# One transformer layer on one core: the opening rewritten in one interleaved order

## What is computed

```python
x = L0_attn_h
xn = _layernorm(x, axis=-1)
x = x + _L0_attn_ref(xn, ...) + _L0_ffn_ref(xn, ...)

# _L0_attn_ref(h, ...)
mu = jnp.mean(h, axis=-1, keepdims=True)
var = jnp.mean(jnp.square(h - mu), axis=-1, keepdims=True)
x = (h - mu) * jax.lax.rsqrt(var + EPS) * ln_g + ln_b
q, k, v = x @ wq.T + bq, x @ wk.T + bk, x @ wv.T + bv   # then rope(q), rope(k)
attn = softmax(causal(q k^T * scale)); o = attn v
return o @ wo.T + bo + residual                         # residual = h

# _L0_ffn_ref(hidden_states, ...)
topk_idx, topk_w = _gate(x, gate_w, gate_bias)          # logits = x @ gate_w.T
out = _moe(x, topk_idx, topk_w, w1, w2, w3)
shared = jax.nn.silu(x @ shared_gate) * (x @ shared_up) @ shared_down
return (out + shared).reshape(b, s, h)
```

## Time and profile before

| | us |
|---|---|
| median of 3 runs | 1180.03 |
| lowest, highest | 1176.62, 1180.87 |
| the profiled execution | 1178.42 |
| its span in the trace | 1176.6 |

### The profile page before, as it was taken

How to read it: one execution, slowest core, us unless ns; L and a number is a source line. 1 busy time by engine, 2 the same in 40 slices (tenths; PEclk the granted TensorE clock), 3 DMA queues, 4 the chain that set the end, 5 groups by cost and what they waited for, 6 DMA issues and landing times.

```text
span 1176.6 us, 18983 instructions
## 1 busy us (share of the span) xinstructions
PE 1076.8 (92%) x6706; PEld 942.2 (80%) x6706; DVE 862.3 (73%) x1691; ACT 665.6 (57%) x1453; POOL 621.7 (53%) x480
## 2 busy tenths in 40 slices
PE   4735789998989999999999999999999999999996
PEld 3635678887778888888888888889888888888885
DVE  6457458898888998887766767676766666676785
ACT  3423456554656655565556656666656566666652
POOL 1045055544555555456475667566665657566541
PEclk9757799998989999999999999999999999999998
DMA  5041021111112211213233323332323223231122
GB/s 178 1 130 59 23 45 37 38 36 46 32 41 45 55 41 42 45 29 77 56 77 77 91 59 78 80 91 65 79 55 85 75 67 77 73 75 33 39 73 90
DMA packets 49613, 73.33 MB, mean 62 GB/s; under 512 B 12272, under 2 KB 26992, under 8 KB 49392
## 3 DMA queue, kind: packets, MB, share of 16 engines
q1 hardware_dynamic: 46192, 67.66, 22.0%
q0 software_dynamic: 3328, 4.46, 2.5%
HBM read 29.74 MB, written 8.80 MB: 33 GB/s over the span
## 4 chain that ended last, share of the span: by engine, by line
PE 79%; DVE 14%; ACT 2%; DMA 2%; issue 1%; POOL 1%; SPq 0%; DVEq 0%; ACTq 0%; POOLq 0%
PE ps L278 22%; PE ps L280 21%; PE ps L279 20%; PE ps L400 10%; PE ps L461 2%; DVE nmax L1246 2%; PE ps L390 1%; PE ps L473 1%; DVE acc L1279 1%; DVE k_l L980 1%; DVE q_l L980 1%; PE ps L319 1%; DMA fin_y<-token_sum 1%; DVE xn L1033 1%; DVE st L1019 1%
## 5 line engine op out<-in xcount | busy, mean ns | idle before, releaser
L1386 POOL TENSOR_TENSOR qb<-qb,k_sb 128x512 f32<-128x512 f32 x128 | 172.5, 1348 | 436.3 <-DMA qs<-qb 436.0
L865 ACT ACTIVATE prob<-ps,nmax 128x128 f32<-128x128 f32 (+7 forms) x256 | 190.5, 744 | 89.4 <-DVE nmax L1246 88.0
L1246 DVE TENSOR_REDUCE nmax<-ps 128x1 f32<-128x128 f32 (+7 forms) x256 | 190.7, 750 | 41.7 <-PE ps L390 40.6
L876 ACT ACTIVATE ptd_h<-ps 128x128 fp32r<-128x128 f32 (+3 forms) x256 | 108.7, 437 | 192.1 <-PE ps L400 191.9
L1390 POOL TENSOR_TENSOR qb<-qb,qs 128x512 f32<-128x512 f32 x128 | 184.7, 1443 | 18.6 <-POOL qs L1387 0.4
L400 PE MATMUL ps<-k_sb,prob 128*128 128x128 f32 x1152 | 178.9, 279 | 11.6 <-DVE ptr_l L1255 6.9
L1255 DVE TENSOR_TENSOR ptd_l<-ps,ptd_h 128x128 fp32r<-128x128 f32 (+3 forms) x256 | 123.8, 484 | 67.3 <-ACT ptd_h L876 65.9
L1387 POOL TENSOR_TENSOR qs<-qs,k_sb 128x512 f32<-128x512 f32 x128 | 172.4, 1347 | 0.0
L400 PEld LDWEIGHTS ps<-k_sb,prob 128*128 128x128 f32 x1152 | 136.4, 144 | 26.5 <-issue 13.3
L278 PE MATMUL ps<-k_h,q_h 128*128 128x512 f32 (+3 forms) x384 | 141.5, 369 | 13.1 <-DVE q_l L980 11.3
L280 PE MATMUL ps<-k_h,q_l 128*128 128x512 f32 (+3 forms) x384 | 133.2, 347 | 0.0
(11 more groups left out here) (163 smaller groups left out, 2735.7 us busy)
## 6 DMA issues: line engine op xcount, KB each, us to landing
qs<-qb SPq DMA_DIRECT2D x256, 128.0 KB, 2.3
ew<-epack SPq DMA_DIRECT2D x16, 768.0 KB
rqk<-wqk SPq DMA_DIRECT2D x16, 256.0 KB, 3.0
xt<-x SPq DMA_DIRECT2D x4, 512.0 KB, 4.9
rv<-wvp SPq DMA_DIRECT2D x8, 256.0 KB, 4.0
ro<-wop SPq DMA_DIRECT2D x16, 128.0 KB, 2.3
token_table<-xn SPq DMA_DIRECT2D x4, 512.0 KB, 4.1
token_sum<-xt SPq DMA_DIRECT2D x4, 512.0 KB, 3.1
```

The source lines that it names most:

```text
L865: act.activation(prob[:, t % 2, 0:w], score[t % 2][:, 0:w], ACT.Exp, bias=nmax[:, t:t + 1], accum_out=rsum[:, t:t + 1]).then_inc(exp_done, 1)
L876: act.activation(turned(0, t, j0, w), src, ACT.Copy).then_inc(pth_done, 1)
L1246: dve.tensor_reduce(nmax[:, t:t + 1], score[t % 2][:, 0:(t + 1) * P], AX.X, ALU.max, negate=True).then_inc(max_done, 1)
L1386: pool.tensor_tensor(qb[:, i, :], qb[:, i, :], cos_sb[:, c], ALU.mult).then_inc(rope_a, 1)
```

## The change

It rewrites the opening. Its parts:

1. *Order.* The stages are cut into pieces (`turn_x`, `turn_z`, `gate`, `shared`, `down` on TensorE; `x_hi`, `again`, `affine`, `z_hi`, `logits`, `shared_tanh`, `shared_hi`, `shared_out` on ScalarE; `stats`, `norm`, `x_lo`, `z_lo`, `shared_g`, `shared_u`, `shared_lo` on VectorE) and written in one interleaved order on all engines, with `pro_uses` to match. The projection of unit 1's first piece moves into it. The closing barrier goes; the scores of unit 0 wait for single banks.
2. *Norm.* The root is made on GpSimd: variance plus eps, power -0.5, a Newton step. `zz` is made on ScalarE as `rstd * xn - mean * rstd`.
3. *No base sum.* GpSimd's `rest` and the stores of the sum go. In unit 1 SP copies the rows of `token_table` to `token_sum` (2048 rows), and ahead of unit 4's rope GpSimd issues an accumulating DMA of x onto them; the first scatter waits for it. `bo` is put in row 0 of `cacc`, which is summed over partitions at the end anyway.
4. *Buffers.* `zz`, `xnh`, `xnl` and `sth` get two places, `sh` and `xnt` go, and statistics have a place for each norm. One of the two buffers of q and k moves in SBUF.
5. *Router product.* It is made of three products on split values (`gwh`, `gwl`), with `xnl` subtracted straight from PSUM.
6. *Loads.* The weights of the shared expert are loaded ahead of the small tables; x's chunks 2 and 3 wait for `xn_ready` alone, and stand ahead of the stores.

```diff
-        pro_uses = stage_a(0) + stage_a(1) + stage_b(0) + stage_a(2) + stage_b(1) + stage_a(3) + stage_b(2) + stage_b(3)
+        pro_uses = [
+            ("xt", 0, 0), ("xt", 0, 1), ("zt", 0, 0), ("zt", 0, 1), ("xt", 1, 0), ("g", 0, 0), ("xt", 1, 1), ("u", 0, 0),
...
+            ("zt", 3, 1), ("gate", 3), ("d", 3, 0), ("d", 3, 1)]
...
                 bank = popen("gate", q)
                 for i in range(GT):
                     for k in range(KC):
-                        ins = pe.matmul(bank[:, i * EXPERTS:(i + 1) * EXPERTS], xnt[:, k, i * P:(i + 1) * P],
-                                        gw[:, k, :], start=(k == 0), stop=(k == KC - 1))
+                        ins = three(pe, bank[:, i * EXPERTS:(i + 1) * EXPERTS],
+                                    (xnh[q % 2][:, k, i * P:(i + 1) * P], xnl[q % 2][:, k, i * P:(i + 1) * P]),
+                                    (gwh[:, k, :], gwl[:, k, :]), k == 0, k == KC - 1)
...
-                if n == 0 and t == 0:
-                    for i in range(4):
-                        pe.wait_ge(pro_free[i], len([u for u in range(len(pro_uses)) if u % 4 == i]))
+                if n == 0 and t in (0, 1, 4, 5):
+                    i = 2 * (t % 2) + t // 4
+                    pe.wait_ge(pro_free[i], len([u for u in range(len(pro_uses)) if u % 4 == i]))
...
             def more_x(q):
-                sp.wait_ge(base_out[q % 2], 16)
+                sp.wait_ge(xn_ready, q - 1)
                 sp.dma_start(xt[:, q % 2, :, :], x_t[q]).then_inc(x_in[q % 2], 16)
 
+            more_x(2)
             rows(0)
             load_rqk(sp, 1)
-            load_ro(sp, 1)
-            more_x(2)
+            more_x(3)
+            rows(1)
             swap(sp, 0, 0)
...
+                if n == 1:
+                    for p in range(2):
+                        sp.wait_ge(rows_out[p], 32)
+                    sp.dma_start(y[0:TOK, :], table[0:TOK, 0:DM]).then_inc(y_rows, 16)
...
+            def again(q):
+                act.wait_ge(root2_ready, q + 1)
+                if q >= 2:
+                    act.wait_ge(pro_done, pcount("zt", q - 2, 1))
+                for i in range(GT):
+                    ins = act.activation(zz[:, q % 2, i, :], xn[:, q % 2, i, :], ACT.Identity, bias=shift[:, q, i:i + 1],
+                                         scale=rstd[:, 2 * q + 1, i:i + 1])
+                ins.then_inc(z_ready, 1)
...
+            def root_of(q, s, nth):
+
+                j = 2 * q + s
+                pool.wait_ge(mv_ready, nth)
+                stepped(pool.tensor_scalar(var[:, j, :], mv[:, j, :, 1], EPS, None, ALU.add))
+                stepped(pool.tensor_tensor(root[:, j, :], var[:, j, :], power[:, :], ALU.pow))
+                stepped(pool.tensor_tensor(newton[:, j, :], root[:, j, :], root[:, j, :], ALU.mult))
+                stepped(pool.tensor_tensor(newton[:, j, :], newton[:, j, :], var[:, j, :], ALU.mult))
+                stepped(pool.tensor_scalar(newton[:, j, :], newton[:, j, :], -0.5, 1.5, ALU.mult, ALU.add))
+                if s == 0:
+                    pool.tensor_tensor(rstd[:, j, :], newton[:, j, :], root[:, j, :], ALU.mult).then_inc(root1_ready, 1)
+                    return
+                stepped(pool.tensor_tensor(rstd[:, j, :], newton[:, j, :], root[:, j, :], ALU.mult))
+                stepped(pool.tensor_tensor(shift[:, q, :], mv[:, j, :, 0], rstd[:, j, :], ALU.mult))
+                pool.tensor_scalar(shift[:, q, :], shift[:, q, :], -1.0, None, ALU.mult).then_inc(root2_ready, 1)
...
+            root_of(0, 0, 1)
+            root_of(1, 0, 2)
+            root_of(0, 1, 3)
+            root_of(1, 1, 4)
+            root_of(2, 0, 5)
+            pool.wait_ge(consts_in, 16)
             rope(pool, 0, 0)
             rope(pool, 0, 1)
-            rest(1)
+            root_of(3, 0, 6)
             rope(pool, 0, 2)
             rope(pool, 0, 3)
-            rest(2)
-            rest(3)
+            root_of(2, 1, 7)
+            root_of(3, 1, 8)
+
+            def base(m):
+                if m != 4:
+                    return
+                pool.wait_ge(y_rows, 16)
+                pool.dma_start(y[0:TOK, :], x, max_dma_last_dim=4 * DM, accum_op=ALU.add).then_inc(y_base, 16)
```

More of the change, by code:

```diff
@@ new lines, in shared @@
+            def shared(q, f, s):
+                for k in range(KC):
+                    pe.wait_ge(*freed("xt", q, k))
+                pe.wait_ge(swl_ready, s + 1)
+                bank = popen("gu"[s], q, f)
+                for k in range(KC):
+                    w = slice(k * FS + f * P, k * FS + (f + 1) * P)
+                    ins = three(pe, bank, (swh[:, s, w], swl[:, s, w]), (xnh[q % 2][:, k, :], xnl[q % 2][:, k, :]),
+                                k == 0, k == KC - 1)
+                ins.then_inc(pro_done, 1)
@@ new lines, in down @@
+            def down(q, i2):
+                pe.wait_ge(shl_ready, 2 * (q + 1))
+                pe.wait_ge(swl_ready, 3)
+                bank = popen("d", q, i2)
+                for i in range(2):
+                    t = slice((2 * i2 + i) * P, (2 * i2 + i + 1) * P)
+                    for f in range(2):
+                        w = slice(f * DM, (f + 1) * DM)
+                        ins = three(pe, bank[:, i * DM:(i + 1) * DM], (shh[:, f, t], shl[:, f, t]),
+                                    (swh[:, 2, w], swl[:, 2, w]), f == 0, f == 1)
+                ins.then_inc(pro_done, 1)
@@ L494, in _ @@
             pe.wait_ge(id_in, 16)
-            pro_a(0)
+            turn_x(0, 0)
+            turn_x(0, 1)
+            turn_z(0, 0)
+            turn_z(0, 1)
+            turn_x(1, 0)
+            shared(0, 0, 0)
+            turn_x(1, 1)
+            shared(0, 0, 1)
+            shared(0, 1, 0)
             project(0, 0)
             project(0, 1)
-            pro_a(1)
-            pro_b(0)
+            gate(0)
+            turn_z(1, 0)
+            turn_z(1, 1)
+            shared(0, 1, 1)
+            turn_x(2, 0)
+            gate(1)
+            turn_x(2, 1)
             project(0, 2)
             project(0, 3)
-            pro_a(2)
-            pro_b(1)
-            for f in range(4):
-                values(0, f)
-            pro_a(3)
-            pro_b(2)
-            pro_b(3)
+            shared(1, 0, 1)
+            shared(1, 0, 0)
+            values(0, 0)
+            shared(1, 1, 0)
+            down(0, 0)
+            down(0, 1)
+            shared(1, 1, 1)
+            values(0, 1)
+            gate(2)
+            shared(2, 0, 0)
+            values(0, 2)
+            project(1, 0)
+            turn_z(2, 0)
+            turn_x(3, 0)
+            shared(2, 1, 0)
+            turn_x(3, 1)
+            shared(2, 0, 1)
+            turn_z(2, 1)
+            shared(2, 1, 1)
+            down(1, 0)
+            down(1, 1)
+            shared(3, 0, 0)
+            shared(3, 1, 0)
+            down(2, 0)
+            down(2, 1)
+            shared(3, 0, 1)
+            shared(3, 1, 1)
+            turn_z(3, 0)
+            turn_z(3, 1)
+            gate(3)
+            values(0, 3)
+            down(3, 0)
+            down(3, 1)
             pe.wait_ge(maskb_ready, 1)
-            pe.wait_ge(pro_act, 1)
-            pe.wait_ge(pro_vec, 1)
-            project(1, 0)
             for n in range(UNITS):
@@ L811, in pro_d, with shared_tanh @@
[L811 to L820 removed]
+            def shared_tanh(q, f):
+                bank = drop("g", q, f)
+                if q:
+                    act.wait_ge(shl_ready, 2 * (q - 1) + f + 1)
+                act.activation(sth[:, f, :], bank, ACT.Tanh, scale=0.5).then_inc(tanh_ready, 1)
@@ L858, in _ @@
-            act.wait_ge(pro_vec, 1)
+            shared_out(3, 0)
+            shared_out(3, 1)
             def exps(n, t):
```

520 lines of the change are left out of this document (274 added, 246 removed), and 4 rows, old and new, of the table pro_uses.

## The result

| | median us | lowest, highest (runs) |
|---|---|---|
| before, measured beside it | 1178.32 | 1175.93, 1180.87 (4) |
| changed | 1116.42 | 1112.83, 1118.84 (4) |

The ratio is 0.9478, 95% interval [0.946, 0.9496]. The forecast was 1118 us, 1.6 above the median; the range held. The profiled execution took 1118.84 us, its span is 1117.0 us.

A forecast was written before the change was run, and what follows sets the result against it. It took the opening to be bound by waits between engines, the rest by TensorE's work. Lead-in 19.9, work 62.2, clock 3 and stalls 6 make 91.1 against 153.5 us, 62.4 less: 1118 us, range 1106 to 1142.

The forecast's parts named there:

- Lead-in: Start of the opening: statistics, two roots and norms until the first eight zz transposes end, at 19.9 us.
- TensorE's work, clock and stalls: Opening behind the lead-in: 62.2 us of work, 3 lost to clock at the stream's start, 6 of stalls (0 to 20).
- What leaves nothing: Removing the opening's base sum gains nothing by itself, its cost being off the new bound; likewise table reloads, barrier, doubled buffers.
- The root is paid once: GpSimd's slower root costs some 4 us at the very start only; later roots lie beside matmuls.
- VectorE 60, ScalarE 54, TensorE 62: Opening's summed work per engine in us; VectorE and ScalarE stay below TensorE's work plus lead-in.
- What comes back later: Units 1 to 4: the 2 MB copy and the 2 MB accumulating DMA, both costed at nothing.
- rival E: Around unit 4's ropes: GpSimd stands inside the accumulating DMA's issue, 88 us more, 1206 us, slower than before; chance 0.03.
- the prediction's own sign of being wrong: Wrong if the first score comes after 115 us, or units 1 to 5 grow by more than 5 us together.
- The rule of the page: Exclusive VectorE-GpSimd port lock: the opening's four ropes could raise VectorE's 60 us to 75, still under 91.
- B: Root chain in the opening is slow, each GpSimd step 1.26 us; 21 us more, 1139 us; chance 0.14.
- C: Opening's pieces do not interlock, 25 us of TensorE idle remain instead of 6; 1137 us; chance 0.13.
- D: Unit 1's copy holds up swaps, all 16 us reaching TensorE through a rope; 1134 us; chance 0.04.

The follow-up runs named there:

- base_behind: Changed kernel with the accumulating DMA of x issued behind unit 4's first rope piece instead of ahead of it; 1111.40 us, ratio 0.9438.
- sum_back: Changed kernel with the base sum and its stores put back into the opening, without the later copy and accumulating DMA; 1129.50 us, ratio 0.9587.
- no_newton: Changed kernel with accumulating DMA moved to unit 12 and copy to unit 9, and the root's Newton step left out; 1111.33 us, ratio 0.9434.
- gate_fp32: Changed kernel with the router's product as eight fp32 matmuls a chunk on xn's high part, instead of 24 on split values; 1110.99 us, ratio 0.9424.
- both_late: Changed kernel with the accumulating DMA moved from unit 4's rope to unit 12's and the token_table copy from unit 1 to 9; 1112.55 us, repeated 1112.27.
- stage_order: Changed kernel with all its parts, but every engine's queue written in the stage order of the kernel before; 1180.31 us, ratio 1.0025.

## Why the forecast was right, and where it was not

*Lead-in.* Forecast 19.9 us to the end of the first zz transposes, measured 21.2. The first root took 2.5 us for the forecast 2.6, but by two errors that cancel: simple steps at 0.28 and the power at 1.13, for 0.44 each. The second took 4.4 instead of 3.5, with wide VectorE operations beside it (0.57 for 0.24, 1.44 for 1.05, 0.63 for 0.24), and the four ScalarE operations behind it 2.07 for 1.6. No extra time for a first call showed: GpSimd starts on mv at 7.12, 0.2 us after it was done.

*TensorE's work, clock and stalls.* Forecast 62.2 + 3 + 6 = 71.2, measured 87.7 - 21.2 = 66.5 without a gap. The router's step was 0.11 as priced. The clock of 0.95 over these 66.5 us is 3.3 us lost, all of it from 30 to 45 us and not at the start of the stream, where the forecast put its 3. At the start the windows give a clock of 1.00, but the matmuls of 512 columns step 0.42 and 0.43 us from 22.46 to 23.31, as at half the clock, for 0.23 later; that is 1.1 us more. With 4.4 lost to the clock for the 3 taken, some 62 are left for the work, as forecast, and no stall at all: the term of stalls was 6 too large. 6 less of stalls against 1.3 more of lead-in and 1.4 more of clock make the 3.3 between 65.7 and 62.4. Stalls and clock were not independent here: in `base_behind`, whose opening is the same program, TensorE stands 1.2 us between 20 and 90 us at a clock of 0.98, and unit 0 starts at 88.13, where the changed kernel has 88.02.

*What leaves nothing.* This step failed, though the sum did not notice it. The prediction put the cost of the base sum on GpSimd and in VectorE's norm, "both off the new bound"; inside the new order, at the places it was given there, the sum costs 16 us at the first score (`sum_back`). It was right only that its removal had already been counted, since I followed the order through without it.

*The root is paid once.* This held for the kernel as it is: TensorE waits for no root behind the lead-in, and shorter chains (`no_newton`) give little more than their two of the lead-in, 2.3 to 3.6 us. It holds without a margin: six more steps a chain cost 11.3 us at the first score, not 4. TensorE is full from 20 to 90 us, but with 1.7 us more a chain chunk 2's norm already comes 2.9 us late. "VectorE 60, ScalarE 54, TensorE 62" compared sums, and a sum does not say that a round of one chunk fits between two places in the order. `gate_fp32` shows the same from the other side.

*What comes back later.* The accumulating DMA was priced at nothing, because GpSimd stands 343 us for swaps over the loop; rival E looked at GpSimd standing inside the issue. The issue took 2.17 us and the transfer 15.1, so rival E is out. What was missed is the third engine: an issue ahead of a rope changes when GpSimd's products run, and VectorE, whose q_l TensorE waits for in unit 2, stands beside them. In the profiled execution that is what the trace shows. That it is the cause of the two groups of times is not shown: the long execution of `base_behind` has no such operation. Units 1 to 5 are 173.8 us against 166.2, that is 7.6 longer, over the 5 that the prediction named as its own refutation; in the execution of 1111.10 us they are 167.0. So the prediction's own sign of being wrong came true in one of the two traced executions, and the term priced at nothing is 1 to 8 us, by execution. That the forecast's 1118 lies only 1.6 above the median of 1116.4 is in part luck: the first score came 3.3 us earlier than forecast, as stalls did not come, and 3.8 us of the 65.7 were given back in the median (6.1 in the profiled execution).

*The rule of the page.* The Trainium skill, SBUF — State Buffer, "SBUF: two separate sides", says that whichever of VectorE (in a two-port mode, or with two inputs in SBUF) and GpSimd starts first holds the port pair they share for the whole instruction. This case's traces agree in their durations (4.15 us beside two rope products, 0.42 alone; 5.25 and 1.38 for the norm), and the rule was used only for the opening. Applied to the loop, it would have named the risk of unit 2. The order of starts doesn't come out of the records: the operation of 4.15 us begins at 169.13, 0.55 us ahead of the first product's record. The traces do not show either why one neighbourhood costs 1 us and another 4.

*The rivals.* B (1.26 us a step) and C (25 us of idle left) are refuted by the trace, and D (the copy holds up swaps by 16 us) by the copy's landing in 8.9 us and by unit 1, which is as long with the copy moved. C's idea is right about the other order: with the same parts and the stage order, TensorE is idle 41.5 of 130 us, for the 51 of 135 before.

*Open.* Why an execution takes one way or the other. Unit 1 already differs (30.1 or 28.4 us) with nearly the same idle time (0.7 and 0.6 us): TensorE is busy 2.46 and 2.57 of the 5 us from 105, and from 110 to 115 the granted clock is 0.50 in one execution,

```profile
110.00:115.00 5.00, 5.00 (x20) 4.35 (x20) 4.71 (x10) 3.81 (x11) 2.98 (x3) 0.50 0.01 3
```

and 0.83 in the other:

```profile
110.00:115.00 5.00, 5.00 (x31) 4.50 (x31) 4.41 (x10) 4.12 (x11) 2.69 (x2) 0.83 0.00 0
```

The shift of 2 us may decide who meets whom in unit 2; that was not tested. Single buffers in the new order were not tried either: with one place for xn's split, by the lists of the order, TensorE would wait for a bank that only its own later work frees. Nor was the new order tried with all of the old parts.

A version faster than both kernels is `both_late`: 1112.3 and 1112.6 us in two measurements, against 1116.4 and 1116.7. `gate_fp32`, at 1110.99, leaves the low part of xn out of the router and was measured once.

## What to carry over

When in-order engines wait for each other in rounds, writing their queues as one interleaved order can decide the gain: here all the other parts together gave nothing without it, and within it a part that was worth 6 us was worth 13. A sum of each engine's work says whether such an order can be full, not how close the next chain is: test the slack by lengthening the chains. And what is moved out of a stage lands beside something: look at which operations of the other engines run there, not only at the slack of the engine and the queue that issue it.

## What was not expected of the hardware

- GpSimd's power of 128x4 takes 1.05 us, its other 128x4 operations 0.19 to 0.24; with a semaphore between them these step 0.28 us. Beside wide VectorE operations they took up to 1.44 and 0.63 in the lead-in.
- A copy of 2 MB from DRAM to DRAM landed in 8.9 us (9.1 to 9.8 in other runs), 1.8 times faster than at the rate of the 512 KB stores. The accumulating DMA of 2 MB landed in 15.1 us (14.9 to 17.3 in other runs), with 2.17 us on GpSimd for the issue.
- A VectorE operation of 0.42 us lasted 4.15 us beside two GpSimd products directly behind a DMA issue, in one traced execution of a kernel and not in the other; in `stage_order` one of 0.69 us lasted 3.94 at the same place.
- The granted clock fell without idle time too: from 30 to 45 us TensorE was busy throughout at 0.87, 0.79 and 0.66 (the router's product ran from 36.6 to 39.5, ahead of the lowest of these). In `base_behind`, with 1.2 us idle from 35 to 45 us in the same program, the clock was 1.00.
